# Ternary weights from sign and magnitude, and the linear attention's mean and variance from rounded and remainder sums

## The chip, the cores and the metric

One NeuronCore of a Trainium2 chip runs the whole program. The metric is device time in microseconds, lower is better. Engines are named as in the profile: PE (TensorE), PEld (its weight loads), DVE (VectorE), ACT (ScalarE), POOL (GpSimd), SP (the queue that issues DMAs).

## The reference

One decoder layer on `x` of 8 batches x 512 tokens x 256 features, three blocks, each followed by a layer norm (mean and variance over the 256 features). Only the first block and the weight part of the third matter here.

```
# block 1: chunked linear attention, chunks of 32 tokens
Q, K, V = x @ W_q.T, x @ W_k.T, x @ W_v.T
S   = (Q K^T within a chunk) * causal decay mask
out = (sigmoid(x @ W_g.T) * (S @ V)) @ W_o.T + x
x   = layernorm(x + out)
# block 2: cross attention, 16 heads, with softmax; layernorm
# block 3: FFN with ternary weights and a low-rank addition; layernorm
scale = clip(mean(|w|, axis=1), 1e-5)
tern  = clip(round(w / scale), -1, 1)              # so +-1 where |w| > scale / 2
h = x @ (tern_fc * scale_fc).T + gate * (x @ v.T @ fast_b.T @ u.T)
y = relu(h)**2 @ (tern_proj * scale_proj).T
```

## The kernel before

Everything is stored transposed: features lie on the 128 partitions in DK = 2 tiles, and the T = 512 tokens of a batch lie along a tile. The program runs the three blocks one after another as phases, each over all B = 8 batches. The order on every engine is written out by hand, with semaphores between engines; there is no planner.

Most matrix products are **split**: an operand `a` is held as `a_hi` (rounded to the type fp32r) and `a_lo = a - a_hi` (also fp32r), and `split_matmul` (L44 to L51) issues hi*hi, lo*hi and hi*lo. `full_matmul` (L54) and single `pe.matmul` calls with float32 operands use the unrounded values; the trace shows two instructions for each of those.

**The linear attention phase** (`linear_attention_phase`, L269) is where the change lies. PE does batch 0 and then `step(b)` for b = 1 to 7 (L770): `gates(b)` (12 split matmuls into G), `variance(b-2)` (one float32 matmul of the 128x128 matrix of 1/D with the tile of summed squares, L719, so that every partition gets the sum), `queries(b)` (12), `outputs(b-1)` (12), `scores(b)` (L57), the first half of `values(b)`, `mean(b-1)` (L715, as `variance`), the second half of `values(b)`, and `attend(b)` (L747). In step 7 both halves of `values` already come before the mean. After step 2 come the scale sums of the FFN weights (`scale_means`), after steps 3 and 4 the low-rank product for one half of the FFN weight each (`low_rank`, L810: two matmuls with 16 rows).

DVE's `step(b)` (L631) is: `finish_y(b-1)` (two residual additions L543 and their sum, L548), `root(b-2)` (L575, L578), `mask_scores(b)` (L567, which `attend` waits for), `scale_x1(b-2)` (L585), `split_x(b+1)` (L501, L503, which `gates(b+1)` waits for), `subtract_mean(b-1)` (L561), `gated(b)` (L592, which `queries(b+1)` and ACT's next sigmoid wait for), `sum_squares(b-1)` (L553), `split_gated(b)` (L598 rounds, L600 takes the remainder; `outputs(b)` waits for both). Behind that, in steps 3 and 4, come `low_rank` (L611) and `compare_in` (L616, L619), and in steps 5 and 6 `compare_out` (L625, L628). A comparison yields `w > scale/2` and `-scale/2 > w`; POOL subtracts the second from the first to get the ternary weight (L414, L423), and for the first FFN weight multiplies by the scale and adds the low-rank part (L416, L418).

ACT does per step: `front(b)` (L436: the sigmoid, with a table load ahead of it and one behind), `query_copies(b)` (L445), `deviation(b-2)` (L463 to L467: Ln, Exp, Square towards the inverse root), `values(b)` (L456), `square(b-1)` (L451). In batches 0 and 1 it also writes |w| of the two FFN weights (L473, L477). POOL splits the cross attention's weights in the first steps (L405, L407), then does the ternary steps, then splits the first inputs of cross attention (L1044 to L1001). SP loads and stores. The cross attention phase follows on every queue; its first instructions on PE are two keys (L1554), then the linear attention's `variance(6)` and, further on, its last outputs, mean and variance.

Of the kernel before, what the change touches and what calls it, by code (L numbers as in the profile page):

```python
# [76 lines left out]
def decoder_layer(nc, a, out):  # L77
    x1_dram = nc.dram_tensor("x1_scratch", [D, B * T], F32, kind="Internal").ap()
    y2_dram = nc.dram_tensor("y2_scratch", [D, B * T], F32, kind="Internal").ap()
    with ExitStack() as whole:  # L80
# [7 lines left out]
        c["mean_w"] = sb(whole, "mean_w", [P, P], F32)  # L88
# [180 lines left out]
def linear_attention_phase(block, ctx, sb, named_sem, a, c, ps, x1_dram):  # L269
# [5 lines left out]
    uT = sb(ctx, "uT", [RANK, HID], F32)  # L275
# [3 lines left out]
    sq = sb(ctx, "sq_a", [P, DK, T], F32)  # L279
# [23 lines left out]
    mid = sb(ctx, "mid", [RANK, D], F32)  # L303
# [16 lines left out]
    above = sb(ctx, "above", [P, DK, HID], BF16)  # L320
    wabs = c["wfc"]

# [16 lines left out]
    f_above, f_below, f_step = sem("f_above"), sem("f_below"), sem("f_step")  # L339
    STAGED, CHUNKS = ("Wq", "Wk", "Wv"), 2 * DK  # L340

# [3 lines left out]
    def _(sp):  # L345
# [16 lines left out]
        sp.dma_start(uT[:], a["uT"]).then_inc(f_in, 16)  # L362
# [32 lines left out]
    def _(pool):  # L395
# [14 lines left out]
        for k in range(DK):  # L410
            n = 3 * k
            pool.wait_ge(f_above, k + 1)
            pool.wait_ge(f_below, k + 1)
            pool.tensor_tensor(wfc[:, k], above[:, k], wfc[:, k], ALU.subtract).then_inc(f_step, 1)  # L414
            pool.wait_ge(f_step, n + 1)
            pool.tensor_tensor(wfc[:, k], wfc[:, k], scale[:], ALU.mult).then_inc(f_step, 1)  # L416
            pool.wait_ge(f_step, n + 2)
            pool.tensor_tensor(c["wfc"][:, k], c["wfc"][:, k], wfc[:, k], ALU.add).then_inc(f_step, 1)  # L418
        for k in range(DK):
            rows = slice(k * HK // DK, (k + 1) * HK // DK)  # L420
            pool.wait_ge(f_above, DK + k + 1)
            pool.wait_ge(f_below, DK + k + 1)
            pool.tensor_tensor(c["tern"][:, rows], c["tern"][:, rows], wpr[:, rows], ALU.subtract).then_inc(f_step, 1)  # L423

    @block.scalar
    def _(act):
# [41 lines left out]

        front(0)
        query_copies(0)  # L470
        values(0)
        act.wait_ge(f_in, 96)
        act.activation(wabs[:], wfc[:], ACT.Abs).then_inc(f_abs, 1)  # L473
        front(1)
        query_copies(1)
        act.wait_ge(f_sum, 1)
        act.activation(wabs[:].rearrange("p k (j n) -> p (k j) n", n=D), wpr[:], ACT.Abs).then_inc(f_abs, 1)  # L477
        values(1)
        square(0)
# [12 lines left out]
    def _(dve):  # L492
# [61 lines left out]

        def subtract_mean(b):
# [1441 lines left out]
```

## Time and profile before

| | |
|---|---|
| median of 3 runs | 1275.84 us (1275.36 to 1276.47) |
| profiled execution | 1275.62 us, of which the profile's span is 1273.6 us |
| PE busy, share of the span | 1256.3 us, 99% |
| PEld busy | 844.5 us, 66% |
| DVE busy | 920.5 us, 72% |
| ACT busy | 794.0 us, 62% |
| POOL busy | 769.9 us, 60% |
| moved from and to HBM | 29.59 MB read, 12.58 MB written |

The linear attention phase takes the first 145.8 us of the span, cross attention about the next 950 us. Busy time says how long an engine had an instruction in it; which engine the others wait for is read from the waits and from the chain that ended last.

### The profile page before, as it was taken

What the parts mean: (1) busy time and instruction counts of PE and PEld (TensorE: products, weight loads), DVE (VectorE), ACT (ScalarE), POOL (GpSimd) and SP (SyncE); (2) the same over time, 40 slices, a digit from 0 to 9 for tenths busy, and PEclk for the clock granted to TensorE, in tenths of its full rate; (3) what the DMA queues carried; (4) which work ended last, traced back from release to release, by engine and by line L of the source; (5) the groups of instructions that cost most, each with busy time, mean ns of one, the idle gap of its engine ahead of it and who ended that gap; (6) DMA issues with size and microseconds to landing.
All of it is one profiled execution on the core that took longest, in us unless ns stands there. A gap on an engine that the chain in (4) does not pass through costs nothing.

```text
span 1273.6 us, 21199 instructions
## 1 busy us (share of the span) xinstructions
PE 1256.3 (99%) x6900; PEld 844.5 (66%) x6900; DVE 920.5 (72%) x1816; ACT 794.0 (62%) x1061; POOL 769.9 (60%) x445
## 2 busy tenths in 40 slices
PE   8999999999999999999999999999999999999997
PEld 6887866666666665756665666657566656777775
DVE  6888877657775778476567756684766777878887
ACT  3444457655665557566656655574656676788885
POOL 3522368967876679487768767795878587200000
PEclk9999999999999999999999999999999999999998
DMA  6311221001100110020011001000100110021101
GB/s 222 116 67 50 69 67 18 4 1 34 37 2 18 33 19 0 17 50 2 0 33 35 1 6 44 19 0 17 39 13 0 34 18 4 24 74 49 50 17 50
DMA packets 99391, 43.08 MB, mean 34 GB/s; under 512 B 77168, under 2 KB 82048, under 8 KB 99344
## 3 DMA queue, kind: packets, MB, share of 16 engines
q1 hardware_dynamic: 98528, 39.33, 12.4%
q0 software_dynamic: 816, 3.15, 0.7%
q8 instruction: 27, 0.44, 0.1%
q14 instruction: 20, 0.16, 0.0%
HBM read 29.59 MB, written 12.58 MB: 33 GB/s over the span
## 4 chain that ended last, share of the span: by engine, by line
PE 92%; POOL 3%; DVE 2%; issue 1%; ACT 1%; DMA 1%; SPq 0%; POOLq 0%; DVEq 0%
PE ps L1425 17%; PE ps L1400 15%; PE ps L48 12%; PE ps L50 11%; PE ps L49 11%; PE ps L1416 4%; PE ps L1404 4%; PE ps L1461 2%; PE ps L1462 2%; PE ps L1460 2%; PE ps L1437 2%; PE ps L1876 2%; PE ps L1875 2%; POOL acc L983 1%; PE ps L747 1%
## 5 line engine op out<-in xcount | busy, mean ns | idle before, releaser
L1216 DVE CUSTOM_DVE_ANT_0 junk<-ps,mask 128x512 bf16<-128x512 f32 x504 | 314.9, 687 | 87.7 <-PE ps L1416 86.4
L1070 ACT ACTIVATE prob<-ps,mcol 128x1024 f32<-128x1024 f32 x256 | 282.2, 1117 | 128.0 <-PE ps L1404 123.5
L983 POOL TENSOR_TENSOR acc<-acc,prob 128x1024 f32<-128x1024 f32 x126 | 300.9, 2388 | 11.5 <-POOL acc L983 0.4
L980 POOL TENSOR_TENSOR acc<-prob 128x1024 f32<-128x1024 f32 x63 | 150.6, 2390 | 193.3 <-ACT prob L1070 192.3
L1425 PE MATMUL ps<-prob,v_b 128*64 128x512 f32 x1024 | 244.5, 598 | 0.0
L997 POOL TENSOR_TENSOR acc_lo<-acc,acc_hi 128x1024 f16<-128x1024 f32 x63 | 136.5, 2166 | 5.0
L1425 PEld LDWEIGHTS ps<-prob,v_b 128*64 128x64 f32 x1024 | 67.8, 136 | 107.1 <-issue 73.7
L1400 PE MATMUL ps<-q_hi,k_hi 64*128 64x512 f32 x512 | 114.1, 441 | 0.2
L1404 PE MATMUL ps<-shift,ones_r 64*128 64x512 f32 x512 | 101.9, 392 | 0.1
L1400 PE MATMUL ps<-q_lo,k_hi 64*128 64x512 f32 x512 | 101.4, 390 | 0.0
L1400 PE MATMUL ps<-q_hi,k_lo 64*128 64x512 f32 x512 | 101.4, 391 | 0.0
L1416 PE MATMUL ps<-k_hi,q_hi 64*128 64x512 f32 x504 | 100.9, 394 | 0.0
L1227 DVE TENSOR_TENSOR ps<-ps,recip 128x512 f32<-128x512 f32 x64 | 44.7, 698 | 69.6 <-ACT recip L1085 69.6
L1077 ACT ACTIVATE pvc<-ps 128x512 f32<-128x512 f32 x64 | 38.4, 600 | 79.4 <-PE ps L1425 79.4
L1240 DVE SCALAR_TENSOR_TENSOR att_lo<-ps,bv,att_hi 128x512 fp32r<-128x512 f32 x64 | 48.0, 750 | 47.3 <-ACT att_hi L1093 47.3
L1400 PEld LDWEIGHTS ps<-q_hi,k_hi 64*128 64x128 f32 x512 | 47.9, 183 | 51.3 <-ACT prob L1070 23.9
L1250 DVE SCALAR_TENSOR_TENSOR q_lo<-ps,bq,q_hi 128x512 fp32r<-128x512 f32 x64 | 48.1, 751 | 31.5 <-ACT q_hi L1101 30.8
L1107 ACT ACTIVATE v_b<-ps 128x512 f32<-128x512 f32 x64 | 38.3, 598 | 50.2 <-PE ps L50 50.2
L1101 ACT ACTIVATE q_hi<-ps,bq 128x512 fp32r<-128x512 f32 x64 | 44.1, 689 | 36.0 <-PE ps L50 36.0
L993 POOL CAST acc_hi<-acc 128x1008 f16<-128x1008 f32 x63 | 64.5, 1024 | 0.0
L1093 ACT ACTIVATE att_hi<-ps,bv 128x512 fp32r<-128x512 f32 x64 | 44.1, 690 | 28.2 <-DVE ps L1235 28.2
L1083 ACT ACTIVATE recip<-ps 128x512 f32<-128x512 f32 x64 | 38.2, 596 | 36.1 <-PE ps L1437 36.1
(265 smaller groups left out, 2927.4 us busy)
## 6 DMA issues: line engine op xcount, KB each, us to landing
shift<-nmx SPq DMA_DIRECT2D x512, 0.5 KB, 2.0
x_in<-in_xT SPq DMA_DIRECT2D x8, 512.0 KB, 3.7
x_scratch<-x_a SPq DMA_DIRECT2D x8, 512.0 KB, 2.9
raw<-in_cT SPq DMA_DIRECT2D x8, 512.0 KB, 3.7
raw<-x_scratch SPq DMA_DIRECT2D x8, 512.0 KB, 3.8
y<-x_scratch SPq DMA_DIRECT2D x8, 512.0 KB, 3.7
y_scratch<-y SPq DMA_DIRECT2D x8, 512.0 KB, 2.8
outT<-x SPq DMA_DIRECT2D x7, 512.0 KB, 2.8
```

Of the source, the lines that this page charges most:

```text
L48: pe.matmul(out, lh, rh, start=(i == 0), stop=False)
L49: pe.matmul(out, lh, rl, start=False, stop=False)
L50: mm = pe.matmul(out, ll, rh, start=False, stop=(i == n - 1))
L980: pool.tensor_tensor(total, prob[:, 0], prob[:, 1], ALU.add).then_inc(acc_out, 1)
L983: pool.tensor_tensor(total, total, prob[:, kt], ALU.add).then_inc(acc_out, 1)
L997: pool.tensor_tensor(acc_lo[:], acc[:], acc_hi[:], ALU.subtract).then_inc(sum_lo_out, 1)
L1070: act.activation(prob[:, i].rearrange("p h t -> p (h t)"), banks.rearrange("p h t -> p (h t)"), ACT.Exp, scale=SCALE, bias=mcol[:, i:i + 1 ...
L1216: dve.tensor_tensor_reduce(junk[:, t % 2, h], SMAX[t % 2][:, h], mask[:], -1.0, -LOWEST, ALU.add, ALU.min, nmx[:, p % 2, t, h:h + 1]).then ...
L1400: pe.matmul(banks[:, h], l[OWN[h], par, cols], r[OWN[h], par], start=(n == 0), stop=False)
L1404: mm = pe.matmul(banks[:, h], ones_r[OWN[h], :], shift[OWN[h], par], start=False, stop=True)
L1416: mm = pe.matmul(SMAX[t % 2][:, h], q_hi[OWN[h], par, toks], k_hi[OWN[h], par], start=True, stop=True)
L1425: mm = pe.matmul(bank[OWN[h], :], v[:, kt, cols], prob[:, kt, h, :], start=(kt == 0), stop=(kt == NT - 1))
```

## The change

The squares' tile `sq` now shares its memory with two new fp32r tiles `sum_hi` and `sum_lo`. Mean and variance of batches 0 to 6 are each made of two fp32r matmuls, of the rounded sum and of its remainder; ACT rounds, DVE subtracts. The mean comes behind all of `values(b)`, the variance behind `queries(b)`. Rounding `og` goes from DVE to ACT. The ternary weight is sign(w) times (|w| > scale/2): ACT makes sign and magnitude, DVE compares once instead of twice, ahead of `split_gated` instead of behind it. The gate times the low-rank product goes from DVE to ACT. The low-rank product's two matmuls read their 16 rows at partitions 0 and 64, for which `uT` is loaded twice and the 16x16 product made twice. ACT's loop over batches is written out. Declarations are left out of the diff where a sentence here says as much.

```diff
@@ -88 +88,2 @@
-        c["mean_w"] = sb(whole, "mean_w", [P, P], F32)
+        c["mean_r"] = sb(whole, "mean_w", [P, P], F32R)
+        c["mean_w"] = f32(c["mean_r"][:])
@@ -279 +280,3 @@
-    sq = sb(ctx, "sq_a", [P, DK, T], F32)
+    with ExitStack() as squares:
+        sq = sb(squares, "sq_a", [P, DK, T], F32)
+    sum_hi, sum_lo = (sb(ctx, n, [P, T], F32R) for n in ("sum_hi_a", "sum_lo_a"))
@@ -362 +366,2 @@
-        sp.dma_start(uT[:], a["uT"]).then_inc(f_in, 16)
+        for rows in RANK_ROWS:
+            sp.dma_start(uT[rows], a["uT"]).then_inc(f_in, 16)
@@ -411,0 +417 @@
+            pool.wait_ge(f_sign, 1)
@@ -413,2 +419 @@
-            pool.wait_ge(f_below, k + 1)
-            pool.tensor_tensor(wfc[:, k], above[:, k], wfc[:, k], ALU.subtract).then_inc(f_step, 1)
+            pool.tensor_tensor(wfc[:, k], sign[:, k], wfc[:, k], ALU.mult).then_inc(f_step, 1)
@@ -417,0 +423 @@
+            pool.wait_ge(f_low, k + 1)
@@ -420,0 +427 @@
+            pool.wait_ge(f_sign, 2)
@@ -422,2 +429 @@
-            pool.wait_ge(f_below, DK + k + 1)
-            pool.tensor_tensor(c["tern"][:, rows], c["tern"][:, rows], wpr[:, rows], ALU.subtract).then_inc(f_step, 1)
+            pool.tensor_tensor(c["tern"][:, rows], c["tern"][:, rows], wpr[:, rows], ALU.mult).then_inc(f_step, 1)
@@ -468,0 +475,20 @@
+        def low_rank(k):
+            act.wait_ge(f_low_ps, k + 1)
+            act.activation(c["wfc"][:, k, :], VY.rearrange("p a n -> p (a n)"), ACT.Identity,
+                           scale=gt[:, 0:1]).then_inc(f_low, 1)
+
+        def round_gated(b):
+            act.wait_ge(gate_used, b + 1)
+            act.wait_ge(y_ps, 2 * b)
+            act.activation(og_hi[:], og[:], ACT.Copy).then_inc(og_rounded, 1)
+
+        def variance_hi(b):
+            act.wait_ge(sq_sum_out, b + 1)
+            act.activation(sum_hi[:], tile_sum[:], ACT.Copy).then_inc(var_hi_out, 1)
+
+        def mean_hi(b):
+            act.wait_ge(y_sum_out, b + 1)
+            if b > 0:
+                act.wait_ge(var_ps, b)
+            act.activation(sum_hi[:], tile_sum[:], ACT.Copy).then_inc(mean_hi_out, 1)
+
@@ -472,2 +498,4 @@
-        act.wait_ge(f_in, 96)
-        act.activation(wabs[:], wfc[:], ACT.Abs).then_inc(f_abs, 1)
+        act.wait_ge(f_in, 112)
+        act.activation(sign[:], wfc[:], ACT.Sign).then_inc(f_sign, 1)
+        act.wait_ge(f_sign, 1)
+        act.activation(wfc[:], wfc[:], ACT.Abs).then_inc(f_abs, 1)
@@ -476,2 +504,4 @@
-        act.wait_ge(f_sum, 1)
-        act.activation(wabs[:].rearrange("p k (j n) -> p (k j) n", n=D), wpr[:], ACT.Abs).then_inc(f_abs, 1)
+        act.activation(c["tern"][:], wpr[:], ACT.Sign).then_inc(f_sign, 1)
+        act.wait_ge(f_sign, 2)
+        act.activation(wpr[:], wpr[:], ACT.Abs).then_inc(f_abs, 1)
+        mean_hi(0)
@@ -480,7 +510,13 @@
-        with act.Fori(2, B - 1, 2) as i:
-            for b in (i, i + 1):
-                front(b)
-                query_copies(b)
-                deviation(b - 2)
-                values(b)
-                square(b - 1)
+        round_gated(1)
+        variance_hi(0)
+        for b in range(2, B):
+            front(b)
+            query_copies(b)
+            deviation(b - 2)
+            mean_hi(b - 1)
+            values(b)
+            square(b - 1)
+            round_gated(b)
+            variance_hi(b - 1)
+            if b in (3, 4):
+                low_rank(b - 3)
@@ -554,0 +591,8 @@
+        def mean_lo(b):
+            dve.wait_ge(mean_hi_out, b + 1)
+            dve.tensor_tensor(sum_lo[:], tile_sum[:], f32(sum_hi[:]), ALU.subtract).then_inc(mean_lo_out, 1)
+
+        def variance_lo(b):
+            dve.wait_ge(var_hi_out, b + 1)
+            dve.tensor_tensor(sum_lo[:], tile_sum[:], f32(sum_hi[:]), ALU.subtract).then_inc(var_lo_out, 1)
+
@@ -595,6 +639,7 @@
-            dve.wait_ge(gate_used, b + 1)
-            if b > 0:
-                dve.wait_ge(y_ps, 2 * b)
-            dve.tensor_copy(og_hi[:], og[:]).then_inc(og_split, 1)
-            dve.wait_ge(og_split, 2 * b + 1)
-            dve.tensor_tensor(og_lo[:], og[:], f32(og_hi[:]), ALU.subtract).then_inc(og_split, 1)
+            if b == 0:
+                dve.wait_ge(gate_used, 1)
+                dve.tensor_copy(og_hi[:], og[:]).then_inc(og_split, 1)
+                dve.wait_ge(og_split, 1)
+            else:
+                dve.wait_ge(og_rounded, b)
+            dve.tensor_tensor(og_lo[:], og[:], f32(og_hi[:]), ALU.subtract).then_inc(og_split, 1 if b == 0 else 2)
@@ -609,5 +653,0 @@
-        def low_rank(k):
-            dve.wait_ge(f_low_ps, k + 1)
-            dve.tensor_scalar(c["wfc"][:, k, :], VY.rearrange("p a n -> p (a n)"), gt[:, 0:1], None,
-                              ALU.mult).then_inc(f_low, 1)
-
@@ -616 +656 @@
-            dve.scalar_tensor_tensor(out=above[:, k], in0=scale[:], scalar=0.5, in1=wfc[:, k],
+            dve.scalar_tensor_tensor(out=wfc[:, k], in0=scale[:], scalar=0.5, in1=wfc[:, k],
@@ -618,3 +657,0 @@
-            dve.wait_ge(f_above, k + 1)
-            dve.scalar_tensor_tensor(out=wfc[:, k], in0=scale[:], scalar=-0.5, in1=wfc[:, k],
-                                     op0=ALU.mult, op1=ALU.is_gt).then_inc(f_below, 1)
@@ -625 +662 @@
-            dve.scalar_tensor_tensor(out=c["tern"][:, rows], in0=bounds, scalar=0.5, in1=wpr[:, rows],
+            dve.scalar_tensor_tensor(out=wpr[:, rows], in0=bounds, scalar=0.5, in1=wpr[:, rows],
@@ -627,3 +663,0 @@
-            dve.wait_ge(f_above, DK + k + 1)
-            dve.scalar_tensor_tensor(out=wpr[:, rows], in0=bounds, scalar=-0.5, in1=wpr[:, rows],
-                                     op0=ALU.mult, op1=ALU.is_gt).then_inc(f_below, 1)
@@ -634,0 +669 @@
+            mean_lo(b - 1)
@@ -642,0 +678,4 @@
+            if b in (3, 4):
+                compare_in(b - 3)
+            if b in (5, 6):
+                compare_out(b - 5)
@@ -643,0 +683 @@
+            variance_lo(b - 1)
@@ -648,6 +687,0 @@
-            if b in (3, 4):
-                low_rank(b - 3)
-            if b in (3, 4):
-                compare_in(b - 3)
-            if b in (5, 6):
-                compare_out(b - 5)
@@ -657 +691 @@
-            dve.tensor_reduce(psc[:], wabs[:].rearrange("p k (j n) -> p n (k j)", n=D), AX.X,
+            dve.tensor_reduce(psc[:], wpr[:].rearrange("p j n -> p n j"), AX.X,
@@ -666 +700 @@
-        dve.tensor_tensor(scale[:], wabs[:, 0], wabs[:, 1], ALU.add).then_inc(f_sum, 1)
+        dve.tensor_tensor(scale[:], wfc[:, 0], wfc[:, 1], ALU.add).then_inc(f_sum, 1)
@@ -668 +702,2 @@
-        dve.tensor_copy(mid[:], ST[0:RANK, 0:D]).then_inc(f_mid, 1)
+        for rows in RANK_ROWS:
+            dve.tensor_copy(mid[rows], ST[rows, 0:D]).then_inc(f_mid, 1)
@@ -710,0 +746,4 @@
+        def sum_parts():
+            pe.matmul(ST, c["mean_r"][:], sum_hi[:], start=True, stop=False)
+            return pe.matmul(ST, c["mean_r"][:], sum_lo[:], start=False, stop=True)
+
@@ -712,2 +751 @@
-            pe.wait_ge(y_sum_out, b + 1)
-            if not (isinstance(b, int) and b == 0):
+            if b > 0:
@@ -715 +753,6 @@
-            pe.matmul(ST, c["mean_w"][:], tile_sum[:], start=True, stop=True).then_inc(mean_ps, 1)
+            if b < B - 1:
+                pe.wait_ge(mean_lo_out, b + 1)
+                sum_parts().then_inc(mean_ps, 1)
+            else:
+                pe.wait_ge(y_sum_out, b + 1)
+                pe.matmul(ST, c["mean_w"][:], tile_sum[:], start=True, stop=True).then_inc(mean_ps, 1)
@@ -718,2 +761,6 @@
-            pe.wait_ge(sq_sum_out, b + 1)
-            pe.matmul(ST, c["mean_w"][:], tile_sum[:], start=True, stop=True).then_inc(var_ps, 1)
+            if b < B - 1:
+                pe.wait_ge(var_lo_out, b + 1)
+                sum_parts().then_inc(var_ps, 1)
+            else:
+                pe.wait_ge(sq_sum_out, b + 1)
+                pe.matmul(ST, c["mean_w"][:], tile_sum[:], start=True, stop=True).then_inc(var_ps, 1)
@@ -771,0 +819 @@
+            queries(b, par)
@@ -774 +821,0 @@
-            queries(b, par)
@@ -781,3 +828 @@
-            values(b, par, (0, 1))
-            if b == B - 1:
-                values(b, par, (2, 3))
+            values(b, par, (0, 1, 2, 3))
@@ -785 +830 @@
-                pe.wait_ge(f_mid, 1)
+                pe.wait_ge(f_mid, 2)
@@ -787,2 +831,0 @@
-            if b < B - 1:
-                values(b, par, (2, 3))
@@ -792,2 +835,4 @@
-            pe.wait_ge(f_in, 96)
-            pe.matmul(ST[0:RANK, 0:D], bT[:], vr[:], start=True, stop=True).then_inc(f_mid_ps, 1)
+            pe.wait_ge(f_in, 112)
+            for rows in RANK_ROWS:
+                mm = pe.matmul(ST[rows, 0:D], bT[:], vr[:], start=True, stop=True)
+            mm.then_inc(f_mid_ps, 1)
@@ -810 +855,2 @@
-                mm = pe.matmul(VY[:, n], mid[:, k * P:(k + 1) * P], uT[:, n * T:(n + 1) * T], start=True, stop=True)
+                mm = pe.matmul(VY[:, n], mid[RANK_ROWS[n], k * P:(k + 1) * P], uT[RANK_ROWS[n], n * T:(n + 1) * T],
+                               start=True, stop=True)
```

## Rows read from the trace of the kernel before

**Rows 1.** The profile page: PE's granted clock in 40 slices, in tenths of full speed

```profile
PEclk9999999999999999999999999999999999999998
```

**Rows 2.** Busy time by stretch: length, PE, PEld, DVE, ACT, POOL, clock, DMA, GB/s

```profile
100.00:120.00 20.00, 18.19 (x101) 14.76 (x100) 18.21 (x17) 9.28 (x12) 7.24 (x3) 1.00 0.16 53
```

**Rows 3.** Timeline of PE: start, length (us), line; one step, from its gates

```profile
129.40 0.47 PE L48 MATMUL ps<-x_hi,WgT_l_hi 128*128 128x512 f32 x1
...
132.23 1.02 PE L719 MATMUL ps<-tile_sum_a,mean_w 128*128 128x512 f32 x2
132.69 0.79 PE L48 MATMUL ps<-x_hi,M_l_hi 128*128 128x512 f32 x1
...
135.85 0.39 PE L48 MATMUL ps<-og_hi,WoT_l_hi 128*128 128x512 f32 x1
...
138.57 1.95 PE L57 MATMUL ps<-qm,x_in 128*128 128x128 f32 x16
...
145.79 0.47 PE L48 MATMUL ps<-bc_hi,wk_hi 128*128 128x512 f32 x1
```

**Rows 4.** The chain of waits by time: start, length, what; matmuls of either kind

```profile
87.80 0.86 PE ps L715 x2
...
94.50 0.23 PE ps L50
```

**Rows 5.** Timeline of PE: the two places in steps 4 and 5 where it stood idle

```profile
107.11 1.10 PE L715 MATMUL ps<-tile_sum_a,mean_w 128*128 128x512 f32 x2 [0.77 <-DVE rs_a L575]
...
112.72 0.50 PE L48 MATMUL ps<-x_hi,WgT_l_hi 128*128 128x512 f32 x1 [0.94 <-DVE x_lo L503]
```

**Rows 6.** Timeline of PE: the low-rank product, and a pair on two array halves

```profile
91.86 1.98 PE L810 MATMUL ps<-uT,mid 16*128 16x512 f32 x4
93.77 0.50 PE L48 MATMUL ps<-x_hi,WgT_l_hi 128*128 128x512 f32 x1
...
187.68 1.08 PE L1425 MATMUL ps<-prob,v_b 128*64 128x512 f32 x4
188.59 0.39 PE L1437 MATMUL ps<-acc_hi,ones_h 128*64 128x512 f16 x2
```

**Rows 7.** Timeline of DVE in step 6, from the split of the next input

```profile
127.50 1.23 DVE L503 TENSOR_TENSOR x_lo<-x_in,x_hi 128x1024 fp32r<-128x1024 f32 x1
128.65 1.21 DVE L561 TENSOR_TENSOR dev_a<-y_a,ps 128x1024 f32<-128x1024 f32 x1
129.78 1.22 DVE L592 TENSOR_TENSOR og_a<-ps,gate 128x1024 f32<-128x1024 f32 x1
130.99 0.69 DVE L553 TENSOR_TENSOR tile_sum_a<-sq_a 128x512 f32<-128x512 f32 x1
...
132.32 1.23 DVE L600 TENSOR_TENSOR og_lo<-og_a,og_hi 128x1024 fp32r<-128x1024 f32 x1
133.46 1.22 DVE L625 SCALAR_TENSOR_TENSOR tern<-psc,wpr_raw 128x1024 bf16<-128x1024 f32 x1
```

**Rows 8.** Timelines of DVE and POOL: instructions of the two that overlap

```profile
23.91 2.19 DVE L600 TENSOR_TENSOR og_lo<-og_a,og_hi 128x1024 fp32r<-128x1024 f32 x1
26.02 1.63 DVE L666 TENSOR_TENSOR scale<-wfc 128x1024 f32<-128x1024 f32 x1
...
24.97 1.60 POOL L405 CAST wq_hi<-raw 128x512 fp32r<-128x512 f32 x1
26.65 2.15 POOL L407 TENSOR_TENSOR wq_lo<-raw,wq_hi 128x512 fp32r<-128x512 f32 x1
...
136.09 2.17 POOL L423 TENSOR_TENSOR tern<-tern,wpr_raw 128x1024 bf16<-128x1024 bf16 x1 [13.89 <-DVE wpr_raw L628]
```

**Rows 9.** Timeline of ACT: square, table load, sigmoid, copy, Ln of a step

```profile
129.90 1.06 ACT L451 ACTIVATE sq_a<-dev_a 128x1024 f32<-128x1024 f32 x1 [1.46 <-DVE dev_a L561]
131.07 1.28 ACT L436 ACT_TABLE_LOAD   x1
132.43 1.02 ACT L436 ACTIVATE gate<-ps 128x1024 f32<-128x1024 f32 x1
...
136.05 0.60 ACT L445 ACTIVATE qm<-ps 128x512 f32<-128x512 f32 x1 [0.68 <-PE ps L50]
```

More of the change, by code:

```diff
@@ L274, in linear_attention_phase @@
     wfc = sb(ctx, "wfc_raw", [P, DK, HID], F32)
-    uT = sb(ctx, "uT", [RANK, HID], F32)
+    uT = sb(ctx, "uT", [P, HID], F32)
     scale = sb(ctx, "scale", [P, HID], F32)
     dev = sb(ctx, "dev_a", [P, DK, T], F32)
-    sq = sb(ctx, "sq_a", [P, DK, T], F32)
+    with ExitStack() as squares:
+        sq = sb(squares, "sq_a", [P, DK, T], F32)
+    sum_hi, sum_lo = (sb(ctx, n, [P, T], F32R) for n in ("sum_hi_a", "sum_lo_a"))
     tile_sum = sb(ctx, "tile_sum_a", [P, T], F32)
@@ L302, in linear_attention_phase @@
     psc = sb(ctx, "psc", [P, D], F32)
-    mid = sb(ctx, "mid", [RANK, D], F32)
+    mid = sb(ctx, "mid", [P, D], F32)
     w_hi["WvT"] = sb(ctx, "WvT_l0_hi", [P, DK, D], F32R)
@@ L319, in linear_attention_phase @@
     gt = sb(ctx, "gt", [P, 1], F32)
-    above = sb(ctx, "above", [P, DK, HID], BF16)
-    wabs = c["wfc"]
+    sign = sb(ctx, "sign", [P, DK, HID], BF16)
     qk_in, gate_w_in = sem("qk_in"), sem("gate_w_in")
@@ L338, in linear_attention_phase @@
     f_ps, f_scale, f_low_ps, f_low = sem("f_ps"), sem("f_scale"), sem("f_low_ps"), sem("f_low")
-    f_above, f_below, f_step = sem("f_above"), sem("f_below"), sem("f_step")
+    f_sign, f_above, f_step = sem("f_sign"), sem("f_above"), sem("f_step")
+    og_rounded, var_hi_out, var_lo_out, mean_hi_out, mean_lo_out = (
+        sem(n) for n in ("og_rounded", "var_hi_out", "var_lo_out", "mean_hi_out", "mean_lo_out"))
     STAGED, CHUNKS = ("Wq", "Wk", "Wv"), 2 * DK
+    RANK_ROWS = (slice(0, RANK), slice(DH, DH + RANK))
     QO, G, VY, S, ST = ps[:, 0:2, :], ps[:, 2:4, :], ps[:, 4:6, :], ps[:, 6, :], ps[:, 7, :]
```

## The prediction

> **What bounds the kernel now.** I read the page first: PE is busy 99% of the span at full clock [rows 1], so a change pays only if it takes time from PE's own queue or from a wait of PE. The whole change lies in the linear attention phase, up to 145.8 us; what follows keeps its code and its PE-bound order, so I carry the shift of its start through to the end one to one. Next the busy time by stretch: in 100 to 120 us PE misses 1.81 us [rows 2], nearly its only idle time between 20 and 145 us. The timeline of PE names its two large pieces: 0.77 us before the mean of step 4 and 0.94 us before the gates of the next step [rows 5]. Then the timeline of one undisturbed step gives PE's budget: gates 129.40 to 132.23, variance and queries to 135.85, outputs to 138.57 [rows 3]; with scores, values, mean and attend the step ends at 145.79 [rows 3], 16.4 us in all. The reader should see there that PE runs without a gap, and in DVE's timeline [rows 7] that the chain x_lo, dev, og, sum of squares, og_lo runs just ahead of PE.
>
> **What the change takes from PE.** (a) A float32 mean or variance occupies PE for 0.86 us, an fp32r matmul of 512 columns for 0.23 [rows 4]. 14 of the 16 become pairs of fp32r: 14 x (0.86 - 0.46) = 5.6 us. (b) The low-rank product takes 1.91 us, 91.86 to 93.77; four instructions that alternate between two halves of the array take 0.91 us, 187.68 to 188.59 [rows 6]. The new one uses two row groups, the row uses column halves. Bounds: 1.91 (nothing gained) and 0.91; I take 0.95, since the form of four float32 instructions is the same. Twice: 1.9 us. (c) The idle 1.8 us of steps 4 and 5 [rows 2, 5] came of POOL's chain reaching DVE's sum and root; the chain now starts earlier in the step, so that place is freed: 1.8 us. The second 16x16 product costs between 0 and 0.5 us (one is 16 columns wide, half as long as a mean); nothing in the sum. Together 9.3 us.
>
> A step of PE alone would then be 16.4 - 0.8 = 15.6 us. Everything else must fit into that.
>
> **What it adds, at no price where covered.** ACT's Sign and second Abs (two of 128x2048 each) fall into steps 0 and 1, where ACT waits for PE; the second DMA of `uT` delays the last of that group by some half microsecond, in front of the same waiting ACT. If Sign brought a table load, 1.28 us each [rows 9], they would still end before the values of step 1. By the Trainium skill (ScalarE: Activation LUTs, Table sets) identity and abs are in every set; Sign is not named there, and no row here shows it. DVE loses the rounding and one comparison and wins two subtractions of 128x512 (0.69 each, as the sum of squares [rows 7]): less work, so DVE's load is no bound. ACT's extra copies are on a ring, below.
>
> **What it adds on the path.** DVE and POOL exclude each other: a remainder of 128x1024 takes 1.23 us [rows 7] but 2.19 us beside POOL, and ends only about 1.1 us after POOL's instruction of 23.41 has ended (25.02). The next row is the one that matters: POOL's cast was issued at 24.97, while DVE held on until 26.10, and then went **first**, until 26.57; DVE's sum, issued at 26.02, was stretched from 1.2 to 1.63 us behind it [rows 8]. So where DVE has two such instructions in a row and POOL is waiting, POOL gets in between. The Trainium skill (SBUF: State Buffer, SBUF: two separate sides) says that a DVE instruction with two SBUF inputs and a GpSimd one that reads SBUF lock each other out whole; the trace agrees with 2.19 against 1.23 us.
>
> (d) In steps 3 to 6 the comparison now stands ahead of og_lo and `variance_lo`. It signals POOL, whose instruction of 2.17 us [rows 8] waits while og_lo runs, goes in between, and holds `variance_lo` back. From the end of og: sum of squares 0.6, comparison 1.15, og_lo 1.15, POOL 2.1, `variance_lo` 0.55, together 5.5 us. PE comes to that variance earlier: gates start when x_lo is there, og ends 2.3 us after x_lo (128.73 to 131.00 [rows 7]), gates and queries take 2.83 + 2.73 [rows 3], so PE stands at the variance 5.6 - 2.3 = 3.3 us behind og. Wait: 2.2 us, and outputs are queued behind it, then everything. Three times in full; the first time, with the low-rank product ahead of the gates and DVE still early, 1.5 us. Sum 3 x 2.2 + 1.5 = 8.1 us. Bounds: 0 (no lock between them: 0.6 + 1.15 + 1.15 + 0.6 = 3.5 us, about PE's own time) and 10.
>
> (e) x_lo is late. From the end of outputs DVE has the second residual, sum, root, now `mean_lo` (0.6), mask, x1, split: before, x_lo ended at 128.73 [rows 7], and that step's scores had started 16.4 us ahead of 138.57 [rows 3], at 122.1: 6.6 us, and 7.2 us now; PE is at the next gates after 1.7 + 2.95 + 0.45 + 1.8 = 6.9 us. 0.35 us in an undisturbed step (two of these), and about 0.6 more where POOL's chain of three stretches DVE's sums: 1.3 us.
>
> (f) Step 7 and its end. POOL's splits of the first cross attention inputs fall, some us earlier than before, on DVE's sum and second root step, and now `mean_lo` stands behind them and the mean, with `attend`, behind that: 1.0 us, between 0 and 2.4 (one POOL subtraction). Behind `attend(7)` there are only two keys, 2.8 us, before `variance(6)`, and none of the usual 5.6; dev, og, ACT's rounding (1.04, as the square [rows 9]), og_lo and `variance_lo` need 5.0 us from the mean and 4.7 from `attend`'s end, so PE waits 1.9 us; the bounds are 0 and 2.5.
>
> (g) In step 1 and 2 POOL splits the wk and wv weights (instructions of 128x512 as in [rows 8]) and gets between og_lo and `variance_lo` in the same way, with 1.2 us each; mostly covered by the 3.3 us; and in step 2 `scales` sits behind that, which outputs of step 3 wait for. 0.5 us, between 0 and 1.7.
>
> **Sum.** Added 8.1 + 1.3 + 1.0 + 1.9 + 0.5 = 12.8, taken away 9.3: 3.5 us more. The same counting applied to the trace of before gives PE waits some 1 us longer than they are in steps 4 to 7, so I take 0.5 us off: +3.0. The profiled execution took 1275.62 us (its span 1273.6 and 2.0 around it), 0.22 us below the median of the runs shown. Forecast 1275.62 + 3.0 = **1278.6 us**, 0.22% over the median of 1275.84, just past what counts as a difference: a measurement of this kernel can tell about 0.2%, 2.55 us, from no change.
>
> **Rivals.**
> 1. **POOL does not get in between (the other side).** DVE's og_lo and `variance_lo` run back to back, and POOL goes after both. For it: the two rows show the alternation for one pair of instructions only, and here the POOL instruction is released by a semaphore from the very comparison ahead. Against it: POOL is waiting 1.1 us before og_lo ends. The 8.1 us shrink to 4 x 0.3, but ACT's ring is then next: from dev, square 1.06 with og beside it, rounding 1.0, variance's copy 0.5, table load 1.3, sigmoid 1.04, table load 1.3, two copies 1.0, Ln to Square 2.0, root 1.4, mean_lo, mask 1.2, x1 1.13, split 1.86, dev 1.2: 16.35 us [rows 7, 9], so 0.7 us a step comes back over some four steps. 3.0 - 8.1 + 1.2 + 2.8 = -1.1: about 1274.5 us; with ACT's ring hidden as well 1271.8. The case decides if PE's wait at the variance is under 0.6 us in steps 4 to 7.
> 2. **PE's savings come through whole**: DVE and ACT keep ahead by more than I count, since each wait is inferred from margins of 0.3 us. 9.3 less about 3 us of waits: 1269.5 us. Against it: the margins in [rows 7] are from the trace.
> 3. **Nothing moves**: gains and waits cancel within 1.5 us, 1276 us. It is my forecast with (d) at 1.2 us instead of 2.2, which it is if the comparison ends later than POOL can use.
> 4. **More waits**: POOL's stretches in (e), (f), (g) at their upper bounds and 0.45 us for the second small product: +4.5 more, 1283 us. PE then idles for over 2 us at a time; the page shows full clock through the idle 1.8 us of 100 to 120 us [rows 1, 2], so I give no clock loss.
>
> **How the numbers follow.** My forecast (1277.3 to 1280.5) 0.42, rival 1 0.18, rival 2 0.10, rival 3 0.20, rival 4 0.10. Faster by over 0.2% (below 1273.3): rival 2 and half of rival 1, 0.19. Within 0.2%: the rest of rival 1, rival 3 and a quarter of the forecast, 0.38. Slower (above 1278.4): 0.43. The range leaves out rival 2's outer part and rival 4's: 1271.8 to 1281.8. As both signs hold much of the chance, the likeliest case's own range is 1277.3 to 1280.5.
>
> **What the next profile would show.** PE's instructions at the mean are two of 0.23 us apart; the low-rank product ends in 0.95 us; steps 1 to 3 start earlier than before (the gates of step 4 at about 73 us against 75.2); from the gates of step 5 on the lead shrinks by some 2 us a step, with PE idle before the variance, released by DVE's `variance_lo`, whose instruction is 2.7 us long instead of 0.7; no idle before a mean in step 4. The forecast is wrong if `variance_lo` is 0.7 us long there, if the cross attention's first instruction starts before 145 us, or if the shift at that point is not the shift at the end.

## The result, and the profile after

The changed kernel takes **1282.66 us** in the median of 6 runs (1279.95 to 1284.81), the kernel before on the same chip 1276.1 us (1275.36 to 1276.55, 6 runs). The ratio is 1.0049, with an interval of 1.0039 to 1.0059: slower by 6 us or so. The sign was forecast. The size was not: the forecast was 1278.6 us, and 1282.66 lies 0.9 us above the upper end of its range (1281.8) and 2.2 us above the range of its likeliest case (1280.5). The profiled execution took 1284.12 us, its span is 1282.1 us, 8.5 us more than before.

The page of the changed kernel: busy time by engine, and PE's granted clock in 40 slices.

```profile
PE 1254.2 (98%) x6902; PEld 845.3 (66%) x6902; DVE 923.8 (72%) x1818; ACT 812.7 (63%) x1085; POOL 770.0 (60%) x445
...
PEclk9999999999999999999999999999999999999999
```

PE's busy time fell by only 2.1 us, where the shorter mean, variance and low-rank product should take 7.3. The clock line gives no reason: a slice is 32 us long, and every slice shows 9. The same trace by stretches of 20 us (length, PE, PEld, DVE, ACT, POOL, clock, DMA, GB/s) does:

```profile
100.00:120.00 20.00, 16.15 (x97) 13.95 (x96) 17.03 (x17) 13.32 (x17) 9.06 (x4) 1.00 0.15 53
120.00:140.00 20.00, 17.66 (x96) 15.12 (x96) 15.48 (x17) 11.21 (x15) 3.53 (x4) 0.91 0.32 105
140.00:160.00 20.00, 18.09 (x94) 15.43 (x95) 12.72 (x16) 8.86 (x14) 7.58 (x5) 0.86 0.09 30
160.00:180.00 20.00, 19.97 (x81) 14.02 (x80) 17.14 (x33) 9.65 (x16) 4.65 (x3) 0.97 0.10 27
```

Two things are to be seen. In 100 to 120 us PE is now idle for 3.85 us, where it was 1.81 [rows 2]. And the clock (seventh value) is below 1.00 in the next three. The first is named by the waits of PE between 20 and 160 us (total, times, longest):

```profile
PE ps L747 <- DVE sum_lo_a L597: 10.0, 6, 2.0
PE ps L48 <- DVE pscale L651: 0.8, 1, 0.8
PE ps L48 <- DVE x_lo L539: 0.7, 2, 0.5
```

10.0 us stand before the variance, which waits for `variance_lo` (L597), and none before a mean. The timeline of PE shows the six, and between them a low-rank product (L855), a mean and gates:

```profile
45.08 0.50 PE L747 MATMUL ps<-sum_hi_a,mean_w 128*128 128x512 f32 x1 [1.30 <-DVE sum_lo_a L597]
...
82.93 0.50 PE L747 MATMUL ps<-sum_hi_a,mean_w 128*128 128x512 f32 x1 [1.23 <-DVE sum_lo_a L597]
...
93.22 1.13 PE L855 MATMUL ps<-uT,mid 16*128 16x512 f32 x4
94.28 0.50 PE L48 MATMUL ps<-x_hi,WgT_l_hi 128*128 128x512 f32 x1
...
101.56 0.50 PE L747 MATMUL ps<-sum_hi_a,mean_w 128*128 128x512 f32 x1 [1.53 <-DVE sum_lo_a L597]
...
109.52 0.40 PE L747 MATMUL ps<-sum_hi_a,mean_w 128*128 128x512 f32 x1
109.75 0.40 PE L748 MATMUL ps<-sum_lo_a,mean_w 128*128 128x512 f32 x1
109.99 1.95 PE L794 MATMUL ps<-s_masked,v_tok 128*128 128x128 f32 x16
...
120.19 0.80 PE L747 MATMUL ps<-sum_hi_a,mean_w 128*128 128x512 f32 x1 [2.02 <-DVE sum_lo_a L597]
120.78 0.63 PE L748 MATMUL ps<-sum_lo_a,mean_w 128*128 128x512 f32 x1
...
140.06 0.50 PE L747 MATMUL ps<-sum_hi_a,mean_w 128*128 128x512 f32 x1 [2.04 <-DVE sum_lo_a L597]
...
156.62 0.50 PE L747 MATMUL ps<-sum_hi_a,mean_w 128*128 128x512 f32 x1 [1.85 <-DVE sum_lo_a L597]
```

What DVE and POOL did ahead of the wait that ends at 120.19:

```profile
114.62 0.69 DVE L589 TENSOR_TENSOR tile_sum_a<-sq_a 128x512 f32<-128x512 f32 x1
115.23 1.22 DVE L662 SCALAR_TENSOR_TENSOR wpr_raw<-psc,wpr_raw 128x1024 f32<-128x1024 f32 x1
116.36 1.22 DVE L645 TENSOR_TENSOR og_lo<-og_a,og_hi 128x1024 fp32r<-128x1024 f32 x1
117.50 2.63 DVE L597 TENSOR_TENSOR sum_lo_a<-tile_sum_a,sum_hi_a 128x512 fp32r<-128x512 f32 x1
...
116.59 2.99 POOL L429 TENSOR_TENSOR tern<-tern,wpr_raw 128x1024 bf16<-128x1024 bf16 x1 [10.37 <-DVE wpr_raw L662]
```

This is term (d) line by line. The comparison (L662) releases POOL's instruction at 116.59, which holds no one up while `og_lo` runs (1.22 us) and then takes the place between `og_lo` and `variance_lo`: 2.63 us for a subtraction that takes 0.69 alone. The Trainium skill (SBUF: State Buffer, SBUF: two separate sides) says that a DVE instruction with two SBUF inputs and a GpSimd one that reads SBUF lock each other out for the whole instruction; the trace agrees, with 1.9 us of 2.63 spent behind POOL.

The clock in stretches of 1 us, around the end of that wait:

```profile
118.00:119.00 1.00, 0.16 (x1) 0.00 (x0) 1.00 (x1) 0.98 (x2) 1.00 (x1) 1.00 0.00 0
...
120.00:121.00 1.00, 0.81 (x2) 0.72 (x3) 0.13 (x1) 0.97 (x2) 0.00 (x0) 0.56 0.00 0
121.00:122.00 1.00, 1.00 (x3) 0.77 (x3) 0.00 (x0) 0.55 (x1) 0.00 (x0) 0.50 0.00 0
122.00:123.00 1.00, 1.00 (x4) 0.74 (x3) 0.00 (x0) 0.94 (x3) 0.00 (x0) 0.50 0.00 0
123.00:124.00 1.00, 1.00 (x5) 0.82 (x4) 0.13 (x1) 0.45 (x1) 0.00 (x0) 0.73 0.00 0
```

Right behind the wait PE works at 0.50, the lower of its two levels (1.2 GHz), for 3.4 us, and a matmul takes 0.63 us in place of 0.40. The same stretch, 3.4 us each time, begins 0.5 us behind the wait that ends at 140.06 and 1.1 us behind the one that ends at 156.62. From the table by 20 us the three cost 20 x (0.09 + 0.14 + 0.03) = 5.2 us of this execution. By the mean granted clock (0.993 to 0.996 in the six runs, 0.997 in most runs of the kernel before) I estimate 3 to 4 us for the median run: less than in the profiled one, which is 1.5 us longer than the median.

**Where the 8.5 us come from.** Cross attention's first shift matmul starts at 171.93 us before and 181.10 after: 9.2 us.

```profile
171.93 0.50 PE L1404 MATMUL ps<-shift,ones_r 64*128 64x512 f32 x2
...
181.10 0.50 PE L1450 MATMUL ps<-shift,ones_r 64*128 64x512 f32 x2
```

From there to the end of the span it is 1101.7 us before and 1101.0 after, so the shift is carried through one to one. Of the 9.2 us: PE's work -5.6 (14 pairs) and -1.7 (the low-rank product, twice 1.91 - 1.06); waits of PE behind the first gates, 11.4 us against 1.9 before: +9.5; clock +5.2; the gates of step 1 start 0.9 us later, at 22.96 against 22.08 (0.5 us of it is there at the first matmul of batch 0, and 0.3 us is a wait for the gate's DMA). That makes 8.3. The rest, 0.9 us, is in PE's busy time: between the first gates and the first shift matmul it fell by 1.2 us (147.84 to 146.64), where 7.3 less and 5.2 more would give 2.1. I put it down to the starts after the nine waits (1.30, 0.79, 1.23, 1.53, 0.48, 2.02, 0.18, 2.04, 1.85), whose first matmul runs 0.50 us instead of 0.40; this is an estimate and not tested by itself.

### The profile page after: what moved, and what is told of

Same layout as the page of the kernel before. It is cut to its first block, busy times and chain, and to the rows that moved or that the text cites. A ratio compares the mean times of both kernels' runs of the same rounds, so it can differ in the third digit from the quotient of the medians.

```text
span 1282.1 us, 21204 instructions
## 1 busy us (share of the span) xinstructions
PE 1254.2 (98%) x6902; PEld 845.3 (66%) x6902; DVE 923.8 (72%) x1818; ACT 812.7 (63%) x1085; POOL 770.0 (60%) x445
## 4 chain that ended last, share of the span: by engine, by line
PE 85%; DVE 6%; issue 3%; POOL 3%; DMA 1%; SPq 1%; ACT 1%; DVEq 0%; POOLq 0%
PE ps L1471 17%; PE ps L1446 15%; PE ps L48 10%; PE ps L50 9%; PE ps L49 9%; PE ps L1450 4%; PE ps L1462 4%; PE ps L1507 2%; PE ps L1506 2%; PE ps L1508 2%; PE ps L1483 2%; PE ps L1921 2%; PE ps L1922 2%; POOL acc L1029 1%; DVE sum_lo_a L597 1%
```

## The experiments

Each ran beside the kernel before, which took 1277.23 us (20 runs) beside the first four.

**Hold POOL back.** POOL's ternary instruction also waits for `variance_lo`.

```diff
             pool.wait_ge(f_above, k + 1)
+            pool.wait_ge(var_lo_out, k + 3)
...
             pool.wait_ge(f_above, DK + k + 1)
+            pool.wait_ge(var_lo_out, k + 5)
```

> The changed kernel, but POOL's ternary instruction that follows each comparison also waits for variance_lo of that step. Theory 1 (POOL gets in between og_lo and variance_lo and holds PE up): variance_lo takes 0.7 us in steps 3 to 6 instead of 2.6, PE's waits before the variance of steps 4 to 7 (1.2 to 2.0 us each) fall under 0.5 us, the half-clock stretches behind them go, and the time falls by 7 to 10 us from the changed kernel's 1282.7, to about 1274. Rival (the chain comparison, og_lo, variance_lo is too long by itself): the waits stay at over 1 us and the time at over 1280.

1279.72 us (12 runs), ratio 1.0023 (1.0013 to 1.0032). DVE and POOL in step 5:

```profile
114.57 1.22 DVE L647 TENSOR_TENSOR og_lo<-og_a,og_hi 128x1024 fp32r<-128x1024 f32 x1
115.71 0.69 DVE L599 TENSOR_TENSOR sum_lo_a<-tile_sum_a,sum_hi_a 128x512 fp32r<-128x512 f32 x1
...
116.56 2.16 POOL L431 TENSOR_TENSOR tern<-tern,wpr_raw 128x1024 bf16<-128x1024 bf16 x1 [10.74 <-DVE sum_lo_a L599]
```

`variance_lo` is back at 0.69 us, and PE no longer waits before the variance in steps 4 to 7. Term (d) is thereby shown, cause and place. The time is not the expected 1274 us: about half of the loss stays (0.23% of 0.49%). At the gates of step 7 this kernel is 2.4 us ahead of the kernel before (126.99 against 129.40 [rows 3]), at the first keys 2.1 us behind (147.92 against 145.79). In between POOL's work is late, and its split of a cross attention input meets `mean_lo` of step 7.

```profile
140.30 2.67 POOL L1049 TENSOR_TENSOR bx_lo<-raw,bx_hi 128x1024 fp32r<-128x1024 f32 x1
...
140.69 2.83 DVE L595 TENSOR_TENSOR sum_lo_a<-tile_sum_a,sum_hi_a 128x512 fp32r<-128x512 f32 x1
...
143.66 0.77 PE L749 MATMUL ps<-sum_hi_a,mean_w 128*128 128x512 f32 x1 [2.73 <-DVE sum_lo_a L595]
...
140.00:144.00 4.00, 1.27 (x9) 1.10 (x9) 3.98 (x3) 1.07 (x2) 2.89 (x2) 0.86 0.00 0
144.00:148.00 4.00, 4.00 (x19) 3.81 (x18) 2.47 (x3) 1.06 (x1) 0.00 (x0) 0.50 0.39 140
```

That is term (f), which the changed kernel itself does not show at its mean: PE waits 2.73 us, and the clock falls while it waits and stays at 0.50 for 6.8 us, until 149.7.

**Comparison behind `variance_lo`.** The three lines with `compare_in` and `compare_out` move behind `variance_lo(b - 1)`.

```diff
-            if b in (3, 4):
-                compare_in(b - 3)
-            if b in (5, 6):
-                compare_out(b - 5)
...
             variance_lo(b - 1)
+            if b in (3, 4):
+                compare_in(b - 3)
+            if b in (5, 6):
+                compare_out(b - 5)
```

> The changed kernel, but DVE's comparison stands behind variance_lo instead of ahead of og_lo. Theory 1: as in the run above, no wait before the variance of steps 4 to 7; POOL starts later and its three instructions for the first weight reach DVE's sum and root of the next step, so some 0.5 to 1.5 us of idle comes before the mean or the gates. Time about 1273 to 1276. Rival (the lock is not what matters, the ring through ACT is): steps take 16.3 us and the time is 1278 or more.

1280.84 us (8 runs), 1.0033 (1.0019 to 1.0046). The waits move once more:

```profile
PE ps L747 <- DVE sum_lo_a L597: 4.4, 2, 3.4
PE ps L747 <- DVE sum_lo_a L593: 2.6, 3, 1.2
```

POOL's chain now ends a microsecond or two later in the step, where it meets sum, root and `mean_lo` (L593), and the last variance, with only two keys as cover, waits 3.4 us (that one released by a `variance_lo` of 0.69 us, so there DVE as a whole is late: its `scale_x1` of step 7 took 2.78 us beside a POOL split). During that wait the clock falls again, to 0.50 for 6.8 us. The time misses the expected 1273 to 1276 us and meets the rival's bound of 1278. For POOL rather than ACT's ring speak the stretched instructions in step 7 (second root step 1.97 us, `mean_lo` 1.52 us), while DVE waited 0.5 us for ACT's rounding; no run separates the two further. In neither order of the comparison is PE free: the split sums put two more instructions of DVE into PE's way, and POOL met one of them each time.

**Work for PE in the wait.** Five more matmuls of 512 columns into ST ahead of the split variance of batches 2 to 6 (from step 4 on), which its first matmul overwrites; they add no result.

```diff
             if b < B - 1:
+                if b > 1:
+                    filler = w_hi["WvT"][:].rearrange("p k n -> p (k n)")
+                    pe.wait_ge(dev_out, b + 1)
+                    for _ in range(5):
+                        pe.matmul(ST, w_hi["WvT"][:, 0, 0:P], filler, start=True, stop=True)
                 pe.wait_ge(var_lo_out, b + 1)
```

> The changed kernel with five more matmuls of 512 columns into the statistics bank in front of each variance of batches 2 to 6; they compute nothing that is used. They cost PE 1.15 us where it does not wait and nothing where it waits 1.2 us or more. Theory (the waits of about 2 us make the clock fall to half for 3.3 to 3.9 us, which costs 5 us): the granted clock stays at 1.00 through 200 us, and the time falls by about 4 us, to 1278 to 1279, with less spread between runs (the changed kernel's six lie 4.9 us apart). Rival (the clock falls for another reason, as the share of busy PE over a longer time): the half-clock stretches stay and the time is the same or up to 2 us more.

1281.64 us (5 runs, all between 1281.21 and 1281.83), 1.0033 (1.002 to 1.0046).

```profile
118.59 1.29 PE L766 MATMUL ps<-WvT_l_hi 128*128 128x512 f32 x5
120.79 0.50 PE L747 MATMUL ps<-sum_hi_a,mean_w 128*128 128x512 f32 x1 [0.91 <-DVE sum_lo_a L597]
...
120.00:140.00 20.00, 18.10 (x105) 15.65 (x106) 16.11 (x17) 12.76 (x18) 4.64 (x5) 1.00 0.32 106
140.00:160.00 20.00, 18.94 (x110) 16.17 (x109) 15.11 (x18) 9.99 (x15) 7.14 (x4) 1.00 0.11 30
```

PE does 25 matmuls more. In this step 5 x 0.23 us of filler and 0.91 us of wait make 2.1 us, as the wait alone did (2.02), and the clock stays at 1.00. From the first gates of step 1 to the first shift matmul it needs 153.4 us, the changed kernel 158.1: 4.7 us less, about the 5.2 us that the clock took there. The changed kernel's second profile (below), with one fall, needs 155.2 us: three, one and no falls fit 1.7 us each. The spread of its times is 0.6 us, against 4.9 us of the changed kernel. So the falls follow PE's idle time, and the profiles agree on what one costs. The expected time, 1278 to 1279 us, was missed: by medians the gain is 1.0 us (1.8 against the later runs), and the intervals of the ratios (1.002 to 1.0046, 1.0039 to 1.0059) overlap, so the size of the gain is not shown by times. Reasons that the profiles give are that the changed kernel doesn't fall three times in each run and that this run waited 1.2 us for the gate's DMA in step 1. The filler shortens both the single waits and their sum; it doesn't tell which of the two counts.

**Sums kept in float32.** Everything of the change but the split: mean and variance are one float32 matmul each again, at their new places; `mean_hi`, `mean_lo`, `variance_hi` and `variance_lo` are gone.

```diff
-            if b < B - 1:
-                pe.wait_ge(var_lo_out, b + 1)
-                sum_parts().then_inc(var_ps, 1)
-            else:
-                pe.wait_ge(sq_sum_out, b + 1)
-                pe.matmul(ST, c["mean_w"][:], tile_sum[:], start=True, stop=True).then_inc(var_ps, 1)
+            pe.wait_ge(sq_sum_out, b + 1)
+            pe.matmul(ST, c["mean_w"][:], tile_sum[:], start=True, stop=True).then_inc(var_ps, 1)
```

> The changed kernel with mean and variance as single float32 matmuls of the unsplit sum again, at the new places; ternary part, low-rank pair and rounding of og on ACT stay as changed. PE gets 5.6 us more work (14 x 0.40) but the variance needs only the sum of squares, 0.6 us behind og. Theory 1: no wait before a variance, no half clock, mask and x_lo are not late; outputs may still wait for og_lo by under 0.5 us. Time 1272 to 1275, below the kernel before, since its 1.8 us of idle and 1.6 us of the low-rank product stay saved. Rival (the ternary and low-rank parts cost by themselves): 1276 or more.

**1272.85 us** (5 runs), 0.9963 (0.9951 to 0.9976).

```profile
100.00:120.00 20.00, 20.00 (x114) 16.74 (x113) 13.16 (x16) 13.04 (x18) 7.37 (x3) 1.00 0.15 53
120.00:140.00 20.00, 20.00 (x129) 17.55 (x128) 15.73 (x20) 10.36 (x13) 9.35 (x7) 1.00 0.32 106
```

PE has no wait at all between 20 and 180 us and full clock. So the split sums, which take 5.6 us from PE's own work, are what makes the change slower; without them the rest of it is a gain of some 4 us, inside the expected 1272 to 1275 us.

**Once more, and the parts alone.** Beside the next four the kernel before took 1276.47 us (35 runs). First the changed kernel itself, unaltered.

> The changed kernel itself once more, on the chip and beside the runs of the kernel before that the others of this call share. Theory: 6 to 7 us over the kernel before, with the same waits before the variance, and with half-clock stretches whose number differs from run to run, which is why its times lie 5 us apart. Rival: the ratio of the first measurement was of that chip alone; here it is within 0.2%.

1283.42 us (12 runs, 1280.32 to 1288.63), 1.005 (1.0033 to 1.0068). From step 4 on the waits before the variance are the same to 0.15 us, with 2.04, 1.98 and 1.83 us for the last three, but its profiled execution (1282.27 us) has one stretch at the lower clock, behind the first of these, not three:

```profile
120.00:140.00 20.00, 17.77 (x96) 15.11 (x96) 15.43 (x17) 11.14 (x16) 3.34 (x4) 0.91 0.32 105
140.00:160.00 20.00, 17.57 (x102) 15.03 (x103) 14.80 (x18) 10.50 (x16) 8.23 (x5) 1.00 0.09 30
```

So a wait of 2 us may bring the fall or not, and this fits the spread: in the first six runs of the changed kernel the mean clock is 0.993 in the longest (1284.81 us) and 0.996 in the shortest (1279.95 us). The clock is not all of it: the longest of the twelve, 1288.63 us, has 0.994 and the shortest, 1280.32 us, 0.996, which by the same reckoning is 2.6 us of 8.3.

**The low-rank pair alone**, put into the kernel before: `uT` and `mid` at partitions 0 and 64, two small products, two matmuls side by side.

```diff
-                mm = pe.matmul(VY[:, n], mid[:, k * P:(k + 1) * P], uT[:, n * T:(n + 1) * T], start=True, stop=True)
+                mm = pe.matmul(VY[:, n], mid[RANK_ROWS[n], k * P:(k + 1) * P], uT[RANK_ROWS[n], n * T:(n + 1) * T],
+                               start=True, stop=True)
```

> The kernel before with nothing but the low-rank pair (second load of uT, second 16x16 product, two row groups). Theory: the pair takes 1.1 us instead of 1.9 twice, 1.6 us off PE; POOL's chain still meets DVE's sum in step 4. The second load comes a little later ahead of the 16x16 product, 0 to 0.5 us. Time 1.0 to 2.0 us under the kernel before. Rival: the idle in step 4 grows by what PE is earlier, and nothing is left: within 0.5 us of the kernel before.

1277.44 us (12 runs), 1.0004 (0.9988 to 1.002): no gain that shows, where 1 to 2 us were expected; the rival holds. The two matmuls do get 0.85 us shorter each time, but PE waits 2.31 us for `x_lo` at the gates of step 6, because DVE's `scale_x1` meets POOL:

```profile
107.77 2.71 POOL L420 TENSOR_TENSOR wfc<-wfc,wfc_raw 128x1024 f32<-128x1024 f32 x1
...
108.76 2.79 DVE L587 SCALAR_TENSOR_TENSOR x_a<-dev_a,rs_a 128x1024 f32<-128x1024 f32 x1
...
100.00:120.00 20.00, 17.69 (x95) 14.81 (x94) 19.14 (x19) 8.68 (x12) 7.57 (x3) 0.91 0.15 53
```

and again the clock is 0.91 in the stretch behind it.

**Variance split only where there is room.** Float32 mean; the variance split only in batches 1 to 5 (`SPLIT = range(1, 6)`), the comparison behind `variance_lo`.

> The changed kernel with a float32 mean, with rounded and remainder sums for the variance of batches 1 to 5 alone, and with DVE's comparison behind variance_lo. Theory: without mean_lo the mask and x_lo are on time; variance_lo is ready about 1.2 us before PE asks for it, POOL is not waiting when it starts, and the two variances with nothing to cover them (batch 0 beside POOL's weight splits, batch 6 behind two keys only) need no remainder. PE work is 2.0 us less than with float32 sums, so the time is 1 to 2 us below that run's, 6 us below the kernel before. Rival: POOL's later chain meets DVE's sums again and PE waits 1 to 2 us in steps 4 and 5: the same time as with float32 sums, or above it.

1274.32 us (12 runs), 0.9985 (0.9969 to 1.0001). PE waits 4.1 us in six places, up to 1.1 us each; the five split variances save 2 us of PE's work and lose more than that against the float32 version that follows. The expected 6 us below the kernel before did not come. (The profiled execution, 1276.89 us, is one of the longer ones; it has a stretch at 0.50 at 11 to 14.4 us, behind a wait of 1.97 us in batch 0.)

**Float32 sums, mean back between the halves of `values`.** The variance stays behind the queries.

> The changed kernel with float32 sums and with the mean back between the halves of the values; the variance stays behind the queries. Theory: the place of the mean alone moves no work of PE and both places are covered when the sums need no remainder, so it is within 0.5 us of the float32 run (4.4 us below the kernel before). Rival (the mean's new place was what freed PE): 1 us or more above that run.

**1272.25 us** (12 runs), 0.9961 (0.9943 to 0.9978), no wait of PE between 20 and 180 us. The mean's place makes no difference that I could measure.

The last three, beside the kernel before at 1276.51 us (25 runs), take the best version apart. The first leaves the low-rank pair out of it, the second also puts the variance back ahead of the queries, which leaves the kernel before with the new ternary weights (with the gate's product and the rounding of `og` on ACT). The third is the best version again.

> The float32 kernel with the mean between the halves of the values, with the low-rank product as before the change too (one row group, one load of uT, one 16x16 product). Theory: PE is the bound and the pair is worth its 2 x 0.85 us of PE time there, so this run is 1.5 to 1.9 us above that kernel, about 2.6 us below the kernel before. Rival: the pair gives nothing, as beside the old ternary part (where the ratio was 1.0004): the same time as that kernel.

> As the run above, with the variance ahead of the queries again: what is left of the change is sign and magnitude with one comparison ahead of split_gated, the gate's product on ACT and the rounding of og on ACT. Theory: the 1.8 us of idle in steps 4 and 5 of the kernel before, and what PE loses in starting again, go with POOL's earlier chain: 2 to 3 us below the kernel before, the same as the run above within 0.5 us, since the variance in float32 has cover at either place. Rival: the variance ahead of the queries comes before its sum and PE waits: above the kernel before.

> The float32 kernel with the mean between the halves once more, beside the two runs above on one chip. 4 to 5 us below the kernel before, PE without a wait from 20 to 150 us, clock 1.00.

Without the pair: 1273.73 us (11 runs), 0.9971 (0.9957 to 0.9985). Ternary part only: 1273.85 us (10 runs), 0.9984 (0.9975 to 0.9993). The best version again: 1273.04 us (9 runs), 0.9977 (0.9966 to 0.9987). The three cannot be told apart by these intervals; by medians the pair is worth 0.7 us, of 1.7 us in PE's work and 1.5 to 1.9 expected, by the ratios nothing, and the place of the variance nothing that shows. From the first gates to the first shift matmul the profiles do show the pair: 145.3 and 145.4 us with it, 147.1 in both without. But with it this part began 1.1 to 1.6 us later, in executions whose first four matmuls of batch 0 took 2.05 us instead of 1.17; that this is the pair's doing is not shown, since of the changed kernel's own two profiles one has it and one has not.

The ternary part alone is faster than the kernel before, clear of the noise: it removes the idle time of steps 4 and 5 (PE busy 20.00 us of 20 in 100 to 120 us, against 18.19 [rows 2]) and adds no wait. The same part of its profile takes 147.05 us against 149.85, 2.8 us less, of which 1.9 us is idle time of PE and 0.9 us busy time: an idle piece of PE cost more here than its own length. This version or either of its neighbours beats both kernels, the changed one by some 10 us.

## Why the prediction was right on the sign and short on the size

- **(a), (b), (c), what PE saves** (9.3 us): right. The pair of fp32r matmuls takes 0.47 us (109.52 to 109.99, against 0.86 [rows 4]); the low-rank product 1.06 (93.22 to 94.28), where I took 0.95; no wait before a mean is left. The second 16x16 product costs nothing: 0.53 us before and 0.54 us after.
- **(d) POOL gets in between**: right in cause, place and length (2.7 forecast, 2.63 measured). PE waits 1.23, 1.53, 2.02 and 2.04 us, 6.8 us against 8.1. Holding POOL back took all four away. Rival 1, that it doesn't get in between, is refuted.
- **(e)** 0.7 us against 1.3. **(f)** The last variance waits 1.85 us, 1.9 forecast. The mean of step 7 waits not at all against 1.0: POOL's last split ended at 146.78 us, and `mean_lo` began at 148.64. Holding POOL back shows the price where it does meet (2.73 us, beyond my bound of 2.4).
- **(g)** mis-sized: 2.1 us against 0.5. ahead of the variance of step 2 DVE waits 0.94 us for ACT's rounding of `og`, and POOL's weight splits stretch `og_lo` to 2.29 us and `variance_lo` to 1.09, so that PE waits 1.30 us; `scales` behind the next one keeps PE another 0.79 us. I had these covered by 3.3 us of slack; they alone pass my bound of 1.7. It also undid the forecast that the gates of step 4 start at about 73 us: 75.95, against 75.22 before.
- **Waits in sum**: 12.8 forecast, 11.4 measured. Without the clock's 5.2 us the profiled execution would have taken 1278.9 us. That this is so near to 1278.6 is in part luck: the waits were 1.4 us under the forecast, and two terms that it puts at nothing, the later start of step 1 and PE's starts after the waits, added 0.9 us each.
- **The step that failed** is the sentence in rival 4, "the page shows full clock through the idle 1.8 us of 100 to 120 us [rows 1, 2], so I give no clock loss". Those 1.8 us were two waits of 0.77 and 0.94 us [rows 5]. I read a sum over 20 us as if it were one wait, and took it as evidence for waits twice as long. Waits of 1.85 to 2.04 us, which my own terms (d) and (f) contained at 2.2 and 1.9 us, were followed by half clock. The loss belonged into the forecast, as a term between 0 and one fall for each such wait; at 5.2 / 3 = 1.7 us each this is 0 to 5 us. The median is 6.6 us above the kernel before where 3.0 were forecast, and the missing 3.6 us is what the mean clock gives for the median run (3 to 4 us, an estimate).
- Rivals 2 and 3 are refuted by 10.0 us of waits before the variance, (d) among them at 1.53, 2.02 and 2.04 us where rival 3 needs 1.2. Rival 4's time, 1283 us, is nearest to the result, but not for its own reason: of its larger stretches only (g)'s came, and the second small product cost nothing.
- The shift at cross attention's start is the shift at the end, as assumed: 9.2 us at 181.10 us, 8.5 us at the end.

Open: what decides if a wait of about 2 us brings the fall of the clock. The two profiles of one kernel differ in it with equal waits. So no run shows that the clock loss of the median run had to come, only that it may.

## What to carry to other kernels

Cutting an engine's own work pays only as long as the others still arrive in time: 5.6 us less of PE's matmuls needed a rounding by ACT and a subtraction by DVE in front of each, and these stood where POOL held DVE up. Before splitting an operand, lay the producer's last instructions beside the consumer's arrival, with every POOL instruction that may be waiting at that time, and price each idle piece of PE by itself: if it is as long as those of 1.8 to 3.4 us here, add what a stretch of 3.4 us at half clock cost (1.7 us), as a term that may come or not. A cheaper way to the same numbers (one comparison less, copies on an idle engine) was worth having here only without the split.

## What the runs showed of the hardware

- **PE's clock after short idle times.** In the changed kernel waits of 1.85, 2.02 and 2.04 us were followed by 3.4 us each at 0.50 of full clock; 1.23, 1.30 and 1.53 us were not. A wait of 2.31 us (pair alone) was followed by 3.4 us too. With waits of 2.73 us (POOL held back) and 3.42 us (comparison behind `variance_lo`) the fall came during the wait and lasted 6.8 us. In the second profile of the changed kernel waits of 1.98 and 1.83 us passed without. It is hidden on the page's clock line of 40 slices.
- **POOL between two instructions of DVE.** With POOL waiting, DVE's 128x512 subtraction behind a 128x1024 one took 2.65, 2.65, 2.63 and 2.63 us in DVE's steps 3 to 6; with POOL held back, 0.68 or 0.69.
- **Sign on ACT** between two sigmoids needed no table load and took as long as the magnitude (1.91 and 1.92 us for 128x2048). The Trainium skill (ScalarE: Activation LUTs, Table sets) has abs in every set; the trace agrees for Abs, which follows without a load:

```profile
22.40 1.91 ACT L499 ACTIVATE sign<-wfc_raw 128x2048 bf16<-128x2048 f32 x1 [2.12 <-DMA gt<-in_gate]
24.34 1.92 ACT L501 ACTIVATE wfc_raw<-wfc_raw 128x2048 f32<-128x2048 f32 x1
```

- **Two 16-row products in different row groups** (partitions 0 and 64) run beside each other, for the 16x16 product (0.54 us for two, 0.53 for one) as for the 512-column ones (1.06 against 1.91 us).
